# Mamba layer with ternary gated MLP: convolution on column halves, first scan column and two gate pairs moved to other engines, new step places

## What is computed

```python
xp, res = jnp.split(layernorm(x) @ W_in.T, 2, axis=-1)          # 512 + 512
xc = silu(causal_depthwise_conv(xp, conv_w, 4 taps) + conv_b)
B, C, dt = split(xc @ W_x.T)                                     # 16, 16, 1
dt = softplus(dt @ W_dt.T + b_dt)                                # 512
h  = exp(A[n] * dt) * h + dt * B[n] * xc                         # over time, 16 states
y  = sum_n C[n] * h[n] + D * xc
x  = x + silu(y + res) @ W_out.T
g  = silu((v @ w1.T) * s1) * ((v @ w2.T) * s2)                   # v = layernorm(x)
x  = x + (gelu(gelu(g @ h1.T * t1) @ h2.T * t2) @ w3.T) * s3
```

## Time and profile before

| | |
|---|---|
| median of 3 runs | 2675.12 us |
| the profiled execution's own time | 2674.63 us |
| its span, first to last instruction | 2672.9 us |
| PE / PE weight loads busy | 2533.8 us (95%) / 2353.8 us (88%) |
| DVE / ACT / POOL busy | 2335.7 us (87%) / 2074.6 us (78%) / 2162.4 us (81%) |
| mean granted TensorE clock | 0.983 of full speed |
| DMA | 199 MB, mean 74 GB/s |

### The profile page before, as it was taken

One profiled execution on the slowest core, in us unless ns is written; L12 is line 12 of the kernel. 1 busy time (PEld: TensorE's weight loads), 2 busy tenths in 40 slices (PEclk: granted clock), 3 DMA queues, 4 the chain that ended last, 5 costly groups with the idle time before them and its releaser, 6 DMA issues. The chain is left out here.

```text
span 2672.9 us, 52818 instructions
## 1 busy us (share of the span) xinstructions
PE 2533.8 (95%) x18562; PEld 2353.8 (88%) x18562; DVE 2335.7 (87%) x2767; ACT 2074.6 (78%) x4560; POOL 2162.4 (81%) x1694
## 2 busy tenths in 40 slices
PE   6679999999999999999999999999987899999999
PEld 5558998898899999998999999999977899999999
DVE  3999999999999999999999999999992377677776
ACT  6887888788887888887888888888776577777774
POOL 3788899999989888899999988888885586666663
PEclk9899999999999999999999999999998999999999
DMA  6111222221222221211212222222131222223330
GB/s 240 37 52 53 70 67 61 68 73 61 63 65 61 72 64 61 75 62 61 80 61 61 68 61 64 71 63 72 62 134 59 73 95 90 93 88 96 95 96 33
DMA packets 130188, 199.02 MB, mean 74 GB/s; under 512 B 16384, under 2 KB 93312, under 8 KB 129920
## 3 DMA queue, kind: packets, MB, share of 16 engines
q1 hardware_dynamic: 129920, 195.57, 23.1%
HBM read 144.68 MB, written 50.86 MB: 73 GB/s over the span
## 5 line engine op out<-in xcount | busy, mean ns | idle before, releaser
L1425 DVE TENSOR_TENSOR_SCAN h<-banks,ub 128x512 f32<-128x512 f32 x1024 | 1197.0, 1204 | 33.6 <-ACT banks L1224 25.1
L874 POOL TENSOR_TENSOR ub<-u,b_row 128x1020 f32<-128x1020 f32 x512 | 1215.5, 2374 | 0.0
L1438 DVE SCALAR_TENSOR_TENSOR acc<-banks,c_tok,acc 128x512 f32<-128x512 f32 x1024 | 714.2, 733 | 28.9 <-PE banks L1773 25.4
L1773 PE MATMUL banks<-ident,h 128*128 128x128 f32 x4096 | 627.3, 277 | 60.0 <-DVE acc L1438 51.9
L1224 ACT ACTIVATE banks<-dt 128x510 f32<-128x510 f32 x1024 | 599.8, 593 | 80.7 <-DVE h L1425 75.2
L1773 PEld LDWEIGHTS banks<-ident,h 128*128 128x128 f32 x4096 | 491.5, 143 | 117.9 <-DVE h L1425 71.6
L1761 PE MATMUL banks<-act_high,h_rounded 128*128 128x256 f32 x2048 | 534.9, 297 | 11.9 <-POOL act_low L901 11.9
L1761 PE MATMUL banks<-act_low,h_rounded 128*128 128x256 f32 x2048 | 504.2, 282 | 0.0
L1761 PEld LDWEIGHTS banks<-act_high,h_rounded 128*128 128x128 f32 x2048 | 390.1, 190 | 12.6 <-issue 12.5
L1761 PEld LDWEIGHTS banks<-act_low,h_rounded 128*128 128x128 f32 x2048 | 390.6, 191 | 0.1
L1747 PE MATMUL banks<-xT_high,w_rounded 128*128 128x256 f32 x1024 | 273.4, 301 | 4.8 <-DVE silu L1410 2.1
(11 more groups left out here) (155 smaller groups left out, 5510.8 us busy)
## 6 DMA issues: line engine op xcount, KB each, us to landing
b_row<-b_scratch SPq DMA_DIRECT2D x128, 512.0 KB, 3.9
z_scratch<-z_out SPq DMA_DIRECT2D x128, 256.0 KB, 3.6
zl_raw<-z_scratch SPq DMA_DIRECT2D x32, 1024.0 KB, 7.3
x_sb<-in_x SPq DMA_DIRECT2D x32, 256.0 KB, 5.0
x_res<-in_x SPq DMA_DIRECT2D x32, 256.0 KB, 4.8
h_full<-in_h SPq DMA_DIRECT2D x2, 4096.0 KB, 17.9
x_scratch<-x_sb SPq DMA_DIRECT2D x32, 256.0 KB, 4.6
out_e<-x_scratch SPq DMA_DIRECT2D x16, 512.0 KB, 3.9
```

What stands on the lines that cost most here:

```text
L874: nc.gpsimd.tensor_tensor(ub[:, n % 2, :, 1:], u[:, :, 1:], b_row[:, n // QUARTER % 2, n % QUARTER:n % QUARTER + 1, 1:].to_broadcast([P, E ...
L1425: nc.vector.tensor_tensor_scan(h[:, n % 2, 2 * i:2 * i + 2].rearrange("p e t -> p (e t)"), banks[:, k % DECAYS, :], ub[:, n % 2, 2 * i:2 * ...
L1438: nc.vector.scalar_tensor_tensor(out=acc[:, par, q], in0=turned[q], scalar=c_tok[:, par, q, n:n + 1], in1=acc[:, par, q], op0=ALU.mult, op ...
L1773: last = nc.tensor.transpose(turned[q][:, e * P:(e + 1) * P], h[:, n % 2, e, q * P:(q + 1) * P], ident[:])
```

## The change

- **Convolution.** `xp` holds each channel tile twice, as two halves `h` of 64 channels. Half `h` has its channels on all 128 partitions: 64 partitions as they come, and 64 with the same channels shifted by one row in time. One matmul contracts two taps at once and gives 64 channels, written to the lower or upper 64 partitions of PSUM. There are still 16 matmuls of 256 columns in a chunk, with 64 weight columns instead of 128, alternating between the halves, in two groups at PE places 0 and 1. ACT copies the straight half in two instructions of 64 partitions each (places 0 and 2), and SP copies it across to the other 64 partitions by two DMAs for each pair of tiles (`cross`).
- **First column.** POOL adds `b_u` to `enter` for 8 states at once; ACT copies the four numbers of a state into `ub` (`first_column`), between the carry and the decays. The add of each state on POOL is gone.
- **Gates.** Pairs 0 and 3: ACT scales the product out of PSUM into `second` (two instructions a pair), POOL multiplies (one of 128x512 a pair). Pairs 1 and 2 stay with DVE, at places 83 and 96.
- **u over xc.** `xc` has two buffers and `u` is written over it, in two halves, as is `dt`.
- **Steps and start.** All tables are new, the checks of the weights are spread over more states, the rate registers are loaded one a state instead of 16 ahead of the first, and the load of `h1` is issued behind the reads of B.

```diff
-        conv_diag = sb("conv_diag", [P, ET, TAPS, P], where=a_only)
+        conv_diag = sb("conv_diag", [P, ET, 2, TAPS // 2, HP], where=a_only)
-        xp = sb("xp", [P, ET, HALO + T], where=a_only)
+        xp = sb("xp", [P, ET, 2, HALO + T], where=a_only)
...
-        DVE_AT = dict(gated=(84, 92, 93, 99))
+        DVE_AT = dict(gated=(83, 96))
-        POOL_AT = dict(low2=27, x1=14, normalize=10, normalize2=22, dt=13, u=15, low=(31, 34, 34, 35))
+        POOL_AT = dict(gate=(29, 33), low2=25, x1=12, normalize=9, normalize2=21, dt=(11, 13), a_dt=15, u=(15, 15), low=(30, 32, 34, 34))
...
-        CHECK_AT = [(0, 1 + k // 2) for k in range(EARLY)] + [(0, 7 + k) for k in range(3)] + [(1, k) for k in range(LATE - 3)]
+        CHECK_AT = [(0, 0), (0, 2), (0, 3), (0, 4), (0, 6), (0, 7), (0, 10), (0, 11), (0, 12), (0, 13), (0, 14), (1, 0), (0, 8), (0, 12), (0, 12), (0, 15), (1, 1), (1, 3), (1, 5), (1, 11), (1, 13), (1, 13)]
...
+            def cross(c, j):
+                rows = slice(2 * j, 2 * j + 2)
+                sp.wait_ge(straight_ready[j], 2 * (c + 1))
+                sp.dma_start(xp[HP:P, rows, 0, HALO - 1:HALO - 1 + T], xp[0:HP, rows, 0, HALO:HALO + T]).then_inc(crossed_in[j], 16)
+                sp.dma_start(xp[0:HP, rows, 1, HALO:HALO + T], xp[HP:P, rows, 1, HALO - 1:HALO - 1 + T]).then_inc(crossed_in[j], 16)
...
-            for name, src in (("w1", w1), ("w2", w2), ("h1", h1)):
+            for name, src in (("w1", w1), ("w2", w2)):
                 sp.dma_start(full[name][:], src.rearrange("(k p) n -> p k n", p=P)).then_inc(early_in, 16)
+            for j in range(2):
+                cross(0, j)
             write_b(0)
             read_b(0, 0)
             read_b(0, 1)
+            sp.dma_start(full["h1"][:], h1.rearrange("(k p) n -> p k n", p=P)).then_inc(h1_in, 16)
...
-                        nc.gpsimd.tensor_tensor(u[:], dt[:, par], xc[:], ALU.mult).then_inc(u_ready, 1)
+                for j in range(2):
+                    if n == POOL_AT["u"][j] and c >= 1:
+                        pool.wait_ge(dt_ready, 2 * c + j + 1)
+                        wait_taken(pool, f"conv{j}", c)
+                        wait_taken(pool, "ssm", c)
+                        for q in range(NT):
+                            wait_full(pool, f"acc{q}", c)
+                        rows = slice(2 * j, 2 * j + 2)
+                        nc.gpsimd.tensor_tensor(u[par][:, rows], dt[:, par, rows], xc[par][:, rows], ALU.mult).then_inc(u_ready, 1)
...
                 pool.wait_ge(enter_ready, 2 * c + half + 1)
+                nc.gpsimd.tensor_tensor(enter[:, rows], enter[:, rows], b_u[:, rows], ALU.add).then_inc(first_ready, 1)
...
-                    nc.gpsimd.tensor_tensor(ub[:, n % 2, :, 0], b_u[:, n], enter[:, n], ALU.add).then_inc(ub_ready, 1)
...
+                for k, p in enumerate(BY_POOL):
+                    if s == POOL_AT["gate"][k]:
+                        wait_taken(pool, f"uu{p}", c)
+                        wait_taken(pool, f"gg{p}", c)
+                        nc.gpsimd.tensor_tensor(silu1[:, p], silu1[:, p], second[:, k % 2], ALU.mult).then_inc(gate_ready, 1)
...
-                take(f"xp{j}", c, xp[:, 2 * j:2 * j + 2, HALO:], bank(f"xp{j}", c).rearrange("p (e t) -> p e t", e=2))
+                wait_full(act, f"xp{j}", c)
+                rows = bank(f"xp{j}", c).rearrange("p (e t) -> p e t", e=2)
+                for half in range(2):
+                    at = HALO - half
+                    last = nc.scalar.activation(xp[HP * half:HP * (half + 1), 2 * j:2 * j + 2, half, at:at + T], rows[HP * half:HP * (half + 1)], ACT.Copy)
+                    last.then_inc(straight_ready[j], 1)
...
+                        for i in range(2):
+                            o = 2 * p + i
+                            last = nc.scalar.activation(second[:, k % 2, i], bank(f"gg{p}", c)[:, i * T:(i + 1) * T], ACT.Copy, scale=scales[:, 1, o:o + 1])
...
+            def first_column(c, n):
+
+                act.wait_ge(first_ready, 2 * c + n // HALF + 1)
+                after(act, scan_done, 2 * (NS * c + n - 1))
+                nc.scalar.activation(ub[:, n % 2, :, 0], enter[:, n], ACT.Copy).then_inc(column_ready, 1)
...
-                    for n in range(NS):
-                        nc.scalar.reg_load(rate[n], neg_a[0:1, n:n + 1].bitcast(I32))
...
+                    first_column(c, n)
+                    if c == 0:
+                        nc.scalar.reg_load(rate[n], neg_a[0:1, n:n + 1].bitcast(I32))
...
                         wait_taken(pe, f"xp{j}", c)
-                        for tap in range(first_tap, first_tap + TAPS // 2):
-                            last = nc.tensor.matmul(into[:, i * T:(i + 1) * T], conv_diag[:, e, tap], xp[:, e, tap:tap + T],
-                                                    start=(tap == 0), stop=(tap == TAPS - 1))
+                        pe.wait_ge(crossed_in[j], 32 * (c + 1))
+                        for i in range(2):
+                            e = 2 * j + i
+                            for b in range(TAPS // 2):
+                                for h in range(2):
+                                    last = nc.tensor.matmul(into[HP * h:HP * (h + 1), i * T:(i + 1) * T], conv_diag[:, e, h, b], xp[:, e, h, 2 * b:2 * b + T],
+                                                            start=(b == 0), stop=(b == TAPS // 2 - 1))
```

More of the change, by code:

```diff
@@ L32 @@
 P = 128
+HP = P // 2
 EPS = 1e-5
@@ L157, in program @@
         z_out = sb("z_out", [P, 2, 2, T], where=a_only)
+        second = sb("second", [P, 2, 2, T], where=a_only)
         a_only.close()
@@ L244, in program @@
         halo_ready = sem("halo_ready")
+        straight_ready = [sem(f"straight_ready{j}") for j in range(2)]
+        crossed_in = [sem(f"crossed_in{j}") for j in range(2)]
+        fold_done = sem("fold_done")
         soft_step = sem("soft_step")
@@ L311, in program @@
+        LAST_PIECE = {"uu": "b", "gg": "b", "h": "d", "xp": "b", "conv": "", "ssm": "b", "acc": "c", "out": "d"}
         MLP_BODIES = 4
@@ L704, in _ @@
                         load_x(to_norm)
+                    for j in range(2):
+                        if n == SP_AT["crossed"][j] and to_front is not None:
+                            cross(to_front, j)
                     if n == SP_AT["write_b"] and to_front is not None:
@@ L828, in front @@
                 par = c % 2
-                if n == POOL_AT["dt"] and c >= 1:
-                    wait_taken(pool, "dtc", c)
-                    pool.wait_ge(soft_step, 3 * c + 3)
-                    nc.gpsimd.tensor_tensor(dt[:, par], dt[:, par], soft[:], ALU.add).then_inc(dt_ready, 1)
-                if n == POOL_AT["u"]:
+                for j in range(2):
+                    if n == POOL_AT["dt"][j] and c >= 1:
+                        wait_taken(pool, "dtc", c)
+                        pool.wait_ge(soft_step, 3 * c + 3)
+                        rows = slice(2 * j, 2 * j + 2)
+                        nc.gpsimd.tensor_tensor(dt[:, par, rows], dt[:, par, rows], soft[:, rows], ALU.add).then_inc(dt_ready, 1)
+                if n == POOL_AT["a_dt"]:
                     if c == 0:
                         pool.wait_ge(a_ready, 2)
-                    pool.wait_ge(dt_ready, c + 1)
+                    pool.wait_ge(dt_ready, 2 * (c + 1))
                     nc.gpsimd.tensor_tensor(a_dt[:, par], dt[:, par, :, 0].rearrange("p (o e) -> p o e", o=1).to_broadcast([P, NS, ET]),
@@ L1060, in project @@
                         wait_full(act, "conv1", c - 1)
-                    nc.scalar.activation(xp[:, :, 0:HALO], xp[:, :, T:T + HALO], ACT.Copy, scale=keep(c)).then_inc(halo_ready, 1)
+                    for k in range(2):
+                        after(act, crossed_in[k], 32 * c)
+                    rows = xp[:].rearrange("p e h t -> p (e h) t")
+                    nc.scalar.activation(rows[:, :, 0:HALO], rows[:, :, T:T + HALO], ACT.Copy, scale=keep(c)).then_inc(halo_ready, 1)
                     act.wait_ge(halo_ready, c + 1)
-                take(f"xp{j}", c, xp[:, 2 * j:2 * j + 2, HALO:], bank(f"xp{j}", c).rearrange("p (e t) -> p e t", e=2))
+                wait_full(act, f"xp{j}", c)
[4 more added lines that the diff above has]
+                    last.then_inc(straight_ready[j], 1)
+                act.wait_ge(straight_ready[j], 2 * (c + 1))
+                act.sem_inc(freed(f"xp{j}", c), 1)
             def front(c, n):
@@ L1149, in silu_conv @@
                         e = 2 * j + i
-                        last = nc.scalar.activation(xc[:, e], bank(f"conv{j}", c)[:, i * T:(i + 1) * T], ACT.Silu, bias=conv_b_sb[:, e:e + 1])
+                        last = nc.scalar.activation(xc[c % 2][:, e], bank(f"conv{j}", c)[:, i * T:(i + 1) * T], ACT.Silu, bias=conv_b_sb[:, e:e + 1])
                     last.then_inc(freed(f"conv{j}", c), 1)
@@ L1401, in mlp @@
             def mlp(c, s):
-                for p in range(PAIRS):
-                    if s == DVE_AT["gated"][p]:
```

(6 more changed lines are left out.)

125 lines of the change are left out of this document (74 added, 51 removed).

## The result

The changed kernel takes **2656.12 us** in the median of 4 runs (2653.20 to 2658.23), the kernel before 2674.76 on the same chip (4 runs). The ratio is 0.993, with a 95% interval of 0.991 to 0.995: the change gains 18.6 us, 0.7%, where 39 were forecast. The profiled execution took 2656.22 us, its span is 18.8 us shorter than that of before.

A forecast was written before the change was run, and what follows sets the result against it. DVE and PE were taken to bound the bodies together. A body of 58.3 + 1.15 + 0.6 + 0.4 = 60.4 us gives -31 us over 30 bodies, the start -7: 2674.6 - 31 - 7 = 2636 us, range 2588 to 2684.

The forecast's parts named there:

- Crossings at the start: Head and first bodies: crossings queue behind 2 MB of weights, made up by the shorter convolution, 0 us.
- the -4 us for chunk 0: Chunk 0: spreading the checks crowded in its first states saves half of 8.3 us, -4 us.
- The convolution: PE in each body: column halves run side by side, 8 matmuls in 1.95 us, saving 3.0 us a body.
- The rival without overlap: Convolution halves don't overlap, PE keeps 60.5 us of work, body at least 62.1 us, 2688 us; chance 0.15.
- The gates: DVE in each body: four gate instructions leave, -1.6 us, bringing its work to 58.3 us.
- POOL's waits at the border: Between bodies: DVE waits for POOL's `ub`, 1.15 us and then 0.6 us a body.
- The wait of 0.6 us later: Behind the border: DVE needs a `ub` at 17.35 us that POOL ends at 17.95, waiting 0.6 us.
- The third thing to look at: DVE should wait for POOL's `ub` or ACT's column once or twice near the border; otherwise body near 59 us.
- First column: In each body: POOL saves 2.4 us and pays 0.5 for two adds; ACT's copies cost +1.9 us.
- The crossing in the body: Start of a body: PE may wait up to 1.2 us for it, covered by DVE's wait for POOL, costed nothing.
- The run-out: Between the last scan and the final PE part: 119 us, unchanged within 3 us either way.

The follow-up runs named there:

- the first two runs above: Changed kernel with `h2` and `w3` loaded behind chunk 1's crossing, 2643.37 us; then also chunk 0's crossing ahead of `w1` and `w2`, 2637.83 us.
- the queue mended: Changed kernel with chunk 0's crossing ahead of `w1`, `w2`; `h1` behind chunk 1's crossing; `h2`, `w3` behind the third quarter of `b`: 2634.59 us.
- the best places tried: Changed kernel with all four gate pairs on DVE, at places 82, 83, 96, 96: 2746.19 us, body 63.36 us.

## Why the prediction was right or wrong

**Right in direction, and the time lies in the range; the forecast was double the gain.** Its own steps, one by one:

*Crossings at the start: this step failed.* The prediction wrote "Crossings at the start queue behind 2 MB of weights, which the shorter convolution makes up for: 0", and for the whole start it took 7 us off: the first scan near 41 us, that of chunk 1 near 102. They came at 46.71 and 128.54. The 2 MB cost chunk 0 about 4 us (the first scan at 45.68 with them ahead and at 41.88 without, in the first two runs above). What the step missed altogether is the crossing of chunk 1, which stands behind 9 MB, and whose lateness goes by way of PE's strict order straight to DVE: 22.16 us. The run with the old convolution, which has no crossing, has its first scans at 40.94 and 101.97, as forecast. So the other terms of the start hold, the -4 us for chunk 0 among them, and the error is the crossings. The best order of the queue brings the scans to 41.85 and 106.70, with 64.85 us between them (65.0 before): the last 4.7 us against the run without crossings stay, 3 of them as DVE's waits behind the late `w3`. From `b_u` to `b_u` chunk 0 of that run is 4.6 us shorter than before, but only because the way from the first `b_u` to the first scan shrank from 8.0 to 3.4 us.

With the queue mended the kernel runs at 2634.6 us against the 2636 forecast, and much of that agreement is luck. Against the kernel before, the stretch up to the first scan of chunk 1 lost 1.7 us (6.5 forecast), the bodies from there to the last `b_u` lost 45.6 (31.5 forecast), and the end grew by 8.0 (0 forecast).

*The convolution: right in its price, not in its count.* 16 records took 1.95 us, as computed. But the computation let a record overlap only with its neighbour in the order, and by the same count the order with four of one half ahead would take 2.8 us; it took 2.00. The rival without overlap is excluded for the changed kernel by one row, and the run with both halves on the same partitions shows what it would have been: 3.67 us a group and a body of 62.6 (rival: 62.1). The Trainium skill, TensorEngine Tiling (Array Packing), section Key Properties, says that different tiles work in parallel, and 1.95 against 3.67 agrees. What the Trainium skill, TensorE: Matmul & The Clock Gate, section The mechanism, says on weight loads of one row group would have made it the rival's case; here the trace disagrees, and the measurement decides. PE's busy time fell by 2.3 us a body instead of 3.0. The groups themselves account for 3.3 (twice 3.62 - 1.95); counted from start to start, with the transposes ahead of them, it is 2.9 (twice 0.44 + 3.46 against 0.59 + 1.88), since a change of width costs some 0.3 us a group, which the prediction had left open (last section). What is between this and the 2.3 I have not traced.

*The gates: the work a little oversized.* DVE's busy time fell by 1.2 us a body, not 1.6, and 1.3 to 1.5 us came back with them. But their undoing costs 3.3 us of body at the best places tried. That DVE and PE both had to be relieved fits: with the old convolution 62.1 us, with the gates back 63.4, both over the 61.4 of before. Both numbers hold for the places of the change, and the second is more place than work.

*POOL's waits at the border: wrong, 1.75 us of the sum.* The prediction had the second `ub` at 9.5 us after its zero and DVE there at 8.35. On that scale (zero at 1024.58 - 1.3 = 1023.28) it ended at 8.66, and DVE came at 8.64. POOL was early by 0.8 us: `u` ended at 1023.77 + 1.30 = 1025.07, 1.8 on this scale, where the count gave -0.2 + 0.3 + 2.5 = 2.6. The whole difference stands ahead of it: the last `ub` of the old body ended at 1019.94 + 2.36 = 1022.30, -1.0 on this scale and not -0.2. The wait of 0.6 us later didn't come either. The third thing to look at said so: "if it doesn't, the body is near 59 us". It is 60.0, between that and the 60.4 forecast: 58.9 us of work (58.3 forecast) and 1.1 us of idle time besides (0.4 forecast), 0.9 of it waits for PE. Two errors of the sum stood against each other, 1.75 us of waits too many and 1.3 us of work and other idle time too few. From chunk 1 to chunk 31 -44.5 us came where -31 was forecast for 30 bodies.

*First column: right.* ACT took it at 54.3 us a body (54.6 forecast), POOL is at 56.2 (55.9), and giving it back costs 1.1 us. The run that gives it back has ACT busy 1.1 us less a body and POOL 1.8 more; 1.9 were forecast for each.

*The crossing in the body: right that it costs nothing, not for the reason given.* PE waited for it 2.7 us in 1000, and it lands after 2.4 us. The waits of DVE for POOL that were to cover it were not there; it wasn't late.

*The run-out: outside its 3 us.* From the last `b_u` the end is 5.4 us later. Windows of after, the last body and the run-out (us, then busy as above, granted clock third from the end):

```profile
1925.24:1991.30 66.06, 50.00 (x354) 46.85 (x352) 60.87 (x71) 50.88 (x116) 51.18 (x32) 0.84 0.34 120
1991.30:2100.40 109.10, 86.52 (x636) 84.24 (x637) 11.98 (x20) 69.06 (x123) 56.24 (x35) 0.89 0.21 71
```

And the same two of before:

```profile
1949.40:2012.40 63.00, 47.55 (x341) 44.10 (x340) 59.42 (x73) 47.68 (x98) 49.41 (x43) 0.87 0.35 128
2012.40:2119.00 106.60, 89.91 (x671) 87.53 (x669) 17.12 (x32) 63.50 (x105) 51.35 (x31) 0.92 0.22 73
```

The last body is 3.1 us longer and the way to the third part 2.5. The granted clock is 0.03 lower in both, and PE waits 16.4 us for `act_low` (11.9 before). The same stretch is 8.0 us longer than before with the queue mended, 8.2 with the old convolution, and 3.2 with the gates back on DVE. No run was made for this part; that it comes from the moved MLP steps, tuned for the body and not for its end, is an argument and not shown.

## What to carry to other kernels

A new small transfer is priced by what stands ahead of it in its queue, not by its size: 128 KB landed in 2.4 us in the bodies and held the kernel for 22 us behind 9 MB of loads that nobody needed yet. So follow each added transfer through the start of the program as well as through its steady state, and put what the next step waits for ahead of bulk loads. Where two engines are both full, test each relief alone: without the shorter convolution the rest of this change lost 18 us in its one run. And a step's work says little until its place is known: two more gate pairs on DVE cost 3.3 to 7.3 us a body, for the same 1.3 to 1.5 us of work.

## What was not expected of the hardware

- Issuing is slow behind large transfers: an issue that takes 0.6 us took 9.32 and 9.68 us behind 8 and 9 MB, and SP issued nothing else meanwhile. With 4 MB ahead (`h2` and `w3` late) the same crossing was issued in 0.60 us, but PE still waited 6.39 us for it.
- Two column halves of 64 ran side by side in either order of their matmuls, 1.95 us and 2.00 us for 16 records, though four of one half stood ahead of the first of the other. On the same output partitions they took 3.67 us.
- Going from full width to halves and back isn't free. The full-width transposes ahead of a group start 0.59 us before it, and the next ones 1.88 us after its start:

```profile
1032.06 0.66 PE L1850 MATMUL banks<-ident,h 128*128 128x128 f32 x4 [1.25 <-DVE h L1499]
...
1034.53 0.66 PE L1850 MATMUL banks<-ident,h 128*128 128x128 f32 x4
```

Compare the rows with both halves on one set of output partitions and those of the old convolution, both shown above. The second group starts 0.59 us after the transposes ahead of it (1013.73 - 1013.14) in the first and 0.44 us (1039.31 - 1038.87) in the second, and the first group takes 3.61 us to the next start (1013.14 - 1009.53) against 3.46 (1038.87 - 1035.41). That is 0.15 us on either side, 0.3 us a group. Whether the second 0.15 us is a pause or 16 slightly slower records the rows don't say.
